# ScalarE copies the last unit's transposed probabilities before, not after, the exponentials of the third slot of a pair

## The chip, the cores and the metric

The kernel runs on one core of one Trainium2 chip. The metric is the device time of one execution, in microseconds (us); lower is better. Three runs of the kernel before took 1274.99, 1270.4 and 1275.39 us, so the median is 1274.99 us.

## The reference, cut to what matters

The input holds 4 sequences of 512 rows with 512 columns. Each goes through a half-weighted feed-forward step, an attention step, and the same feed-forward step again:

```python
x = x + 0.5 * ffn(layernorm(x))     # W_base, plus low-rank experts weighted by a softmax
x = x + attention(layernorm(x))
x = x + 0.5 * ffn(layernorm(x))

# attention, 32 heads, causal, latent width 64
scores = (q_lat @ c_kv.T + q_rope @ k_rope.T) / sqrt(192)    # lower triangle only
probs = softmax(scores)
out = (probs @ c_kv) @ w_uv[h]      # per head, then concatenated
return out @ w_out
```

Nearly all of the time is in the attention step. All of it is float32 in and out; the kernel computes most products from a high and a low part of each operand.

## The kernel before, in words

For each of the four sequences (the loop variable `b`; the first three run in a hardware loop, the fourth is written out after it), `attend` works through 16 pairs of heads, then `last_outputs` and `steps` do the rest. The scores of one pair of heads make five **units** (`MEMBERS`), each of at most 512 columns of one PSUM bank: unit 0 and unit 1 are the last 128 rows of head 0 and head 1 (512 columns each), units 2 and 3 are 384 + 128 columns of one head each, and unit 4 is 256 + 256 columns, one of each head. So a sequence has 80 **slots** `u`, five to a pair, with `k = u % 5`. I call the slot with k = 2 the third slot, and the one with k = 3 the fourth.

What one unit goes through: TensorE computes its scores (`scores`, L849 to L851); VectorE adds the mask and takes the negated maximum (L1490); ScalarE takes the exponentials and their sum (L1120); VectorE inverts the sum (`inverse_sums`, L1445); GpSimd multiplies the unit's probabilities by it (L576); three slots later (`T_LAG = 3`) TensorE transposes the unit into a PSUM bank (`transpose_probs`, L870); and ScalarE or VectorE copies that bank to `probT` in SBUF (`copy_probT`: L367 on ScalarE for units 0, 2 and 4, L369 on VectorE for units 1 and 3). Because of the lag of three slots, unit 4 of a pair is transposed and copied in the third slot of the next pair, beside that pair's unit 2. In the fourth slot TensorE multiplies all of the pair's `probT` by `ckv` (`pv`, L885, 20 matmuls).

All engines run their instructions in the order written, and wait on semaphores. In the third slot the orders are:

- TensorE: scores of unit 2; the query products of head 1 of the next pair (`q_products`, L834); the transposes of the old unit 4. In the fourth slot: scores of unit 3; `pv`; the transposes of unit 0. In the fifth: scores of unit 4, transposes of unit 1, and six matmuls of the output projection (`output`, L911).
- ScalarE: `qT_high` (L1091, the high part of the next queries of head 0); the exponentials of unit 2; the copy of the old unit 4. In the fourth slot: exponentials of unit 3, copy of unit 0.
- VectorE: mask and maximum of unit 2, `inverse_sums` of unit 1, three products for the rotary embedding of the queries (L1436 to L1438). In the fourth slot: mask of unit 3, then `inverse_sums` of unit 2.
- GpSimd: `q_sum` (L496), scaling of unit 2 (L576); in the fourth slot `qT_low` (L501) and the scaling of unit 3.

The waits that matter here. `pv` waits for all five copies of its pair (`probT_by_act`, `probT_by_dve`) and for `oT_hi_set` and `oT_lo_set` of the pair before. The copy waits for `probT_done`, which the last transpose of the unit sets, and for `pv_done` of the pair before. The exponentials of unit `u` wait for `neg_max_set` (VectorE) and for the transposes of unit `u - 4`, whose buffer they overwrite. The scores of unit `u + 2` wait for the exponentials of unit `u` (`prob_set`), whose PSUM bank they overwrite. The exponentials' instructions are one ACTIVATE and one ACTIVATION_READ_ACCUMULATOR per member of the unit.

Of the kernel before, what the change touches and what calls it, by code (L numbers as in the profile page):

```python
# [58 lines left out]
UNITS = 5  # L59
# [13 lines left out]
T_LAG = 3  # L73
# [6 lines left out]
ACT_BANKS = (0, 2, 4)  # L80
# [27 lines left out]
def build(nc, hidden, w_q_down, w_q_up_nope, w_q_up_rope, w_kv_down, w_k_rope, w_uk, w_uv, w_out,  # L108
          W_base, b_base, lora_A, lora_B, router_W, router_b, domain_prior, active,
          rope_cos, rope_sin, rope_cosT, rope_sinT, out):  # L110
    with ExitStack() as ctx:
# [206 lines left out]
        def attention(slot_work, tail):  # L318

            for g in range(BODIES):  # L320
                for u in range(BODY + (tail if g == BODIES - 1 else 0)):
                    slot_work(g, u)

        def known(g, u, least):

            return not isinstance(g, int) or BODY * g + u >= least

        def within(g, u, most):

            return not isinstance(g, int) or BODY * g + u <= most  # L330
# [15 lines left out]
        def probT_unit(v):  # L346

            k = v % UNITS
            if k == UNITS - 1:
                return probT[:].rearrange("p (h s) q -> p h s q", h=2)[:, :, 2:6:3, :]  # L350
            at = HEAD_BLOCKS * (k % 2) + k // 2
            return probT[:, at:at + 10:3, :]

        def bank_unit(v):

            if v % UNITS == UNITS - 1:
                return probT_ps[v % 2].rearrange("p (h s q) -> p h s q", h=2, s=2)
            return probT_ps[v % 2].rearrange("p (s q) -> p s q", s=4)

        def copy_probT(eng, do, b, g, v):  # L360

            pair = 16 * b + BODY_PAIRS * g + v // UNITS
            eng.wait_ge(probT_done, 80 * b + BODY * g + v + 1)
            if known(g, v, UNITS):
                eng.wait_ge(pv_done, pair)
            if eng.engine == nc.scalar.engine:
                do.activation(probT_unit(v), bank_unit(v), ACT.Copy).then_inc(probT_by_act, 1)  # L367
            else:
                do.tensor_copy(probT_unit(v), bank_unit(v)).then_inc(probT_by_dve, 1)  # L369
# [4 lines left out]
        def q_index(b, n, head):  # L374

            return 34 * b + 2 + 2 * n + head

        SLOTS = UNITS * PAIRS
        LAST_PAIR = PAIRS - 1

        with nc.Block() as block:
# [574 lines left out]
            def _(act):  # L956
# [132 lines left out]
                def qT_high(m, head, par, cols=slice(0, S)):  # L1089
                    act.wait_ge(q_sum_set, m + 1)  # L1090
                    nc.scalar.activation(qT_hi[par][:, head, cols], q_sums[par][:, head, cols],  # L1091
                                         ACT.Copy).then_inc(qT_hi_set, 1)

                def oT_high(b, g, p):

                    q = p - 2
                    act.wait_ge(pv_done, 16 * b + BODY_PAIRS * g + q + 1)
                    if q % 2 == 0 and known(g, UNITS * q, 4 * UNITS):
                        act.wait_ge(y_ps, 32 * b + ST * ((BODY_PAIRS // 2) * g + q // 2 - 1))
                    elif q % 2 == 1 and known(g, UNITS * q, 3 * UNITS):  # L1100
                        act.wait_ge(y_ps, 32 * b + ST * ((BODY_PAIRS // 2) * g + q // 2))
                    nc.scalar.activation(oT_hi[oT_buffer(q)][:], o_ps, ACT.Copy).then_inc(oT_hi_set, 1)

                def attend(b):
                    def work(g, u):
                        k, p = u % UNITS, u // UNITS
                        n1 = BODY_PAIRS * g + p + 1
                        queries = within(g, u, UNITS * LAST_PAIR - 1)
                        if k == 0 and known(g, u, 2 * UNITS):
                            oT_high(b, g, p)  # L1110
                        if k in (2, 4) and queries:
                            qT_high(q_index(b, n1, k // 2 - 1), k // 2 - 1, (p + 1) % 2)
                        if within(g, u, SLOTS - 1):
                            n = 80 * b + BODY * g + u
                            act.wait_ge(neg_max_set, n + 1)
                            if known(g, u, RING):
                                act.wait_ge(probT_done, n - RING + 1)
                            for m, (_, i, c) in enumerate(MEMBERS[k]):
                                w = (i + 1) * P
                                last = nc.scalar.activation(prob[u % RING][:, c:c + w], score_ps[u % 2][:, c:c + w],  # L1120
                                                            ACT.Exp, bias=neg_max[:, u % RING, m:m + 1], scale=-1.0,
                                                            accum_out=row_sum[:, u % RING, m:m + 1])
                            last.then_inc(prob_set, 1)
                        v = u - T_LAG
                        if known(g, u, T_LAG) and within(g, u, SLOTS - 1 + T_LAG) and v % UNITS in ACT_BANKS:
                            copy_probT(act, nc.scalar, b, g, v)
                    attention(work, TAIL)

# [410 lines left out]
```

## Time and profile before

| What | Value |
|---|---|
| Median of the three runs | 1274.99 us |
| The profiled execution's own time | 1273.67 us |
| Its span, first to last instruction | 1271.8 us |
| Mean granted TensorE clock | 0.969 of full speed |
| TensorE matmul (PE) busy | 1132.7 us (89%) |
| VectorE (DVE) busy | 935.7 us (74%) |
| ScalarE (ACT) busy | 597.7 us (47%) |
| GpSimd (POOL) busy | 740.3 us (58%) |

The page calls TensorE's matmuls PE, its weight loads PEld, VectorE DVE, ScalarE ACT and GpSimd POOL; L885 is line 885 of the kernel. The attention steps of the four sequences take roughly 400 to 620 us, and so on: one such step is about 210 us long, and its 16 `pv` are 14 us apart for most of it. A busy share says little by itself: the matmuls' ends are modelled, and a matmul overlaps the next by about 0.16 us, so that two matmuls with nothing between them stand in the trace with a slightly negative gap. The idle time before an instruction is given in square brackets, with who ended it.

### The profile page before, as it was taken

The numbers are of one execution on the slowest core, as the hardware profiler recorded it, in microseconds if no ns is written. First come the engines' busy times: TensorE is split into PE (matmuls) and PEld (weight loads), VectorE is DVE, ScalarE is ACT, GpSimd is POOL, SyncE is SP. The second block draws the span as 40 slices with busy tenths as digits, with TensorE's granted clock in tenths as the row PEclk, the third lists the DMA queues.
The fourth block names the chain that finished last, engine by engine and source line by source line (L and its number), as shares of the span: only waits on it lengthen the run. The fifth ranks groups of instructions, "written<-read, shape, count | busy, mean of one in ns | idle before, by whom it ended". The sixth has DMA issues, their size and how long they took to land.

```text
span 1271.8 us, 24129 instructions
## 1 busy us (share of the span) xinstructions
PE 1132.7 (89%) x7312; PEld 935.6 (74%) x7312; DVE 935.7 (74%) x3049; ACT 597.7 (47%) x1698; POOL 740.3 (58%) x943
## 2 busy tenths in 40 slices
PE   5978899999897899999887889999989689999996
PEld 4646777777695777777686677777769567777776
DVE  4767778886676877887667777788667668878855
ACT  3645555555133555555323455555512355555541
POOL 1417877776214877777303777777721387777741
PEclk9999999999898999999989999999989899999998
DMA  9740000000100000000100000000000000000000
GB/s 264 204 137 1 2 1 1 2 1 2 33 34 2 2 1 1 2 1 1 35 34 2 1 2 1 1 1 1 1 34 34 2 1 1 2 1 1 1 1 34
DMA packets 21674, 28.00 MB, mean 22 GB/s; under 512 B 10247, under 2 KB 12039, under 8 KB 20907
## 3 DMA queue, kind: packets, MB, share of 16 engines
q1 hardware_dynamic: 19178, 21.71, 5.5%
q10 hardware_dynamic: 2368, 4.72, 1.2%
q8 instruction: 65, 1.06, 0.4%
q14 instruction: 63, 0.51, 0.1%
HBM read 22.23 MB, written 4.19 MB: 21 GB/s over the span
## 4 chain that ended last, share of the span: by engine, by line
PE 50%; DVE 20%; issue 16%; ACT 6%; POOL 5%; SPq 1%; DMA 1%; DVEq 0%; ACTq 0%; POOLq 0%
PE Y L885 10%; PE Y L911 9%; PE XZ L870 6%; PE Y L616 5%; PE XZ L616 4%; PE Y L834 3%; DVE XZ L1490 3%; DVE q_turned L1437 3%; ACT prob L1120 3%; DVE q_sums L1436 3%; DVE probT L369 2%; PE XZ L849 2%; ACT probT L367 2%; PE XZ L851 2%; PE XZ L850 2%
## 5 line engine op out<-in xcount | busy, mean ns | idle before, releaser
L1120 ACT ACTIVATE prob<-XZ,small 128x512 f32<-128x512 f32 (+3 forms) x512 | 266.5, 525 | 344.3 <-DVE small L1490 343.9
L576 POOL TENSOR_TENSOR prob<-prob,small 128x512 f32<-128x512 f32 (+3 forms) x512 | 360.3, 721 | 63.6 <-DVE small L1445 47.1
L1490 DVE CUSTOM_DVE_ANT_0 XZ<-XZ,mask 128x512 f32<-128x512 f32 (+3 forms) x512 | 245.1, 510 | 162.3 <-issue 160.0
L496 POOL TENSOR_TENSOR q_sums<-q_sums,q_turned 64x512 f32<-64x512 f32 (+2 forms) x136 | 165.2, 1215 | 163.4 <-DVE q_turned L1438 159.6
L501 POOL TENSOR_TENSOR qT_lo<-q_sums,qT_hi 128x512 fp32r<-128x512 f32 (+2 forms) x136 | 166.0, 1221 | 79.6 <-ACT qT_hi L1091 79.6
L870 PE MATMUL XZ<-ident,prob 128*128 128x128 f32 x1280 | 196.0, 276 | 5.1 <-POOL prob L576 4.8
L885 PE MATMUL Y<-probT,ckv 128*64 128x384 f32 (+2 forms) x1280 | 155.6, 390 | 48.0 <-ACT probT L367 48.0
L849 PE MATMUL XZ<-kT_hi,qT_hi 128*128 128x512 f32 (+3 forms) x512 | 178.5, 349 | 17.3 <-POOL qT_lo L501 11.2
L870 PEld LDWEIGHTS XZ<-ident,prob 128*128 128x128 f32 x1280 | 150.2, 140 | 44.1 <-issue 14.4
L885 PEld LDWEIGHTS Y<-probT,ckv 128*64 128x64 f32 x1280 | 92.1, 139 | 105.6 <-issue 62.9
L850 PE MATMUL XZ<-kT_lo,qT_hi 128*128 128x512 f32 (+3 forms) x512 | 166.9, 326 | 0.0
L851 PE MATMUL XZ<-kT_hi,qT_lo 128*128 128x512 f32 (+3 forms) x512 | 166.7, 326 | 0.0
L367 ACT ACTIVATE probT<-XZ 128x512 f32<-128x512 f32 x192 | 114.6, 597 | 63.2 <-PE XZ L870 62.3
L849 PEld LDWEIGHTS XZ<-kT_hi,qT_hi 128*128 128x128 f32 x512 | 98.1, 192 | 27.6 <-ACT prob L1120 11.3
L1449 DVE TENSOR_TENSOR x_sb<-Y,x_sb 128x512 f32<-128x512 f32 x128 | 88.0, 687 | 35.1 <-PE Y L911 34.3
L911 PE MATMUL Y<-wo_hi,oT_hi 128*128 128x512 f32 x256 | 110.9, 433 | 1.6 <-DVE x_sb L1449 1.4
L470 POOL TENSOR_TENSOR var_eps<-moments,small 128x1 f32<-128x1 f32 (+3 forms) x26 | 5.2, 201 | 176.7 <-DVE moments L1152 176.7
L850 PEld LDWEIGHTS XZ<-kT_lo,qT_hi 128*128 128x128 f32 x512 | 98.7, 193 | 5.0
L851 PEld LDWEIGHTS XZ<-kT_hi,qT_lo 128*128 128x128 f32 x512 | 98.1, 192 | 5.7
L1120 ACT ACTIVATION_READ_ACCUMULATOR prob<-XZ,small 128x1 f32 x512 | 100.8, 197 | 1.0 <-issue 1.0
L911 PE MATMUL Y<-wo_hi,oT_lo 128*128 128x512 f32 x256 | 101.0, 395 | 0.0
L911 PE MATMUL Y<-wo_lo,oT_hi 128*128 128x512 f32 x256 | 100.3, 392 | 0.0
(199 smaller groups left out, 2300.2 us busy)
## 6 DMA issues: line engine op xcount, KB each, us to landing
wout_nat<-in_L_attn_w_out_dram SPq DMA_DIRECT2D x16, 512.0 KB, 4.3
out_dram<-x_sb SPq DMA_DIRECT2D x16, 256.0 KB, 2.0
x_next<-_attn_hidden_states_dram SPq DMA_DIRECT2D x12, 256.0 KB, 3.6
wbase_nat<-in_L_ffn_W_base_dram ACTq DMA_DIRECT2D x1, 1024.0 KB, 5.4
x_sb<-_attn_hidden_states_dram ACTq DMA_DIRECT2D x4, 256.0 KB, 6.8
nope_a<-_L_attn_w_q_up_nope_dram ACTq DMA_DIRECT2D x1, 1024.0 KB, 7.0
rope_a<-_L_attn_w_q_up_rope_dram SPq DMA_DIRECT2D x1, 1024.0 KB, 8.8
rope_bb<-_L_attn_w_q_up_rope_dram SPq DMA_DIRECT2D x2, 512.0 KB, 11.4
```

Of the source, the lines that this page charges most:

```text
L367: do.activation(probT_unit(v), bank_unit(v), ACT.Copy).then_inc(probT_by_act, 1)
L496: nc.gpsimd.tensor_tensor(q, q, turned, ALU.add).then_inc(q_sum_set, 1)
L501: nc.gpsimd.tensor_tensor(qT_lo[par][:, head, cols], q_sums[par][:, head, cols], f32(qT_hi[par][:, head, cols]), ALU.subtract).then_inc(qT ...
L576: last = nc.gpsimd.tensor_tensor(prob[u % RING][:, c:c + w], prob[u % RING][:, c:c + w], inv_sum[:, u % RING, m:m + 1].broadcast_to([P, w] ...
L849: nc.tensor.matmul(bank[:, c:c + w], high, kT_hi[:, 0:w], start=True, stop=False)
L850: nc.tensor.matmul(bank[:, c:c + w], high, kT_lo[:, 0:w], start=False, stop=False)
L851: last = nc.tensor.matmul(bank[:, c:c + w], low, kT_hi[:, 0:w], start=False, stop=True)
L870: last = nc.tensor.transpose(probT_ps[v % 2][:, at], prob[v % RING][:, at], ident[:])
L885: last = nc.tensor.matmul(o_ps[64 * h:64 * h + 64, column * P:(column + n) * P], ckv[:, j, :], probT[:, HEAD_BLOCKS * h + at:HEAD_BLOCKS * ...
L911: last = nc.tensor.matmul(bank, o[buffer][:, rows], w, start=(k == 0 and j == 0), stop=(k == 1 and j == 2))
L1120: last = nc.scalar.activation(prob[u % RING][:, c:c + w], score_ps[u % 2][:, c:c + w], ACT.Exp, bias=neg_max[:, u % RING, m:m + 1], scale= ...
L1490: last = nc.vector.tensor_tensor_reduce(bank, bank, mask[:, S - w:S], -1.0, HIGHEST, ALU.add, ALU.min, neg_max[:, u % RING, m:m + 1])
```

## The change

In `attend` of ScalarE the condition for the copy is computed before the exponentials. If the slot is a third slot (k = 2), the copy is issued there, before the exponentials of unit 2; in the other slots that have one (k = 0 and k = 3) it stays behind the exponentials. Nothing else is changed: the same instructions with the same waits are issued, and only ScalarE's order of two of them in 15 of the 16 third slots of each sequence differs (the first third slot has no copy; the one after the last pair has no exponentials).

```diff
                         if k in (2, 4) and queries:
                             qT_high(q_index(b, n1, k // 2 - 1), k // 2 - 1, (p + 1) % 2)
+                        v = u - T_LAG
+                        copies = known(g, u, T_LAG) and within(g, u, SLOTS - 1 + T_LAG) and v % UNITS in ACT_BANKS
+                        if copies and k == 2:
+                            copy_probT(act, nc.scalar, b, g, v)
                         if within(g, u, SLOTS - 1):
                             n = 80 * b + BODY * g + u
                             act.wait_ge(neg_max_set, n + 1)
...
                             last.then_inc(prob_set, 1)
-                        v = u - T_LAG
-                        if known(g, u, T_LAG) and within(g, u, SLOTS - 1 + T_LAG) and v % UNITS in ACT_BANKS:
+                        if copies and k != 2:
                             copy_probT(act, nc.scalar, b, g, v)
```

## Rows read from the trace of the kernel before

**Rows 1.** Chain of waits, 445 to 475 us: start us, us, what it was.

```profile
458.99 0.49 ACT probT L367
459.49 0.23 issue
459.71 2.38 PE Y L885 x20
...
463.83 1.41 PE Y L911 x6
465.26 0.05 DVE x_sb L1449
...
471.95 0.19 DVE XZ L1490
...
473.98 1.05 PE Y L885 x7
```

**Rows 2.** Who waited for whom, whole span: us in total, times, longest.

```profile
PE Y L885 <- ACT probT L367: 48.0, 60, 1.8
```

**Rows 3.** The same view, 418 to 626 us (second sequence).

```profile
PE Y L885 <- ACT probT L367: 12.4, 15, 1.4
```

**Rows 4.** The same view, 1028 to 1234 us (fourth sequence).

```profile
PE Y L885 <- ACT probT L367: 10.8, 15, 1.8
```

**Rows 5.** Timeline of PE, 457.5 to 463: start us, us, instruction, [idle before <-releaser].

```profile
457.61 0.60 PE L870 MATMUL XZ<-ident,prob 128*128 128x128 f32 x4
...
458.74 0.27 PE L851 MATMUL XZ<-kT_hi,qT_lo 128*128 128x128 f32 x1
459.71 2.38 PE L885 MATMUL Y<-probT,ckv 128*64 128x384 f32 x20 [0.70 <-ACT probT L367]
462.02 0.66 PE L870 MATMUL XZ<-ident,prob 128*128 128x128 f32 x4
```

**Rows 6.** Timeline of ACT, 457 to 463.

```profile
456.65 0.62 ACT L1091 ACTIVATE qT_hi<-q_sums 128x512 fp32r<-128x512 f32 x1
457.97 0.58 ACT L1120 ACTIVATE prob<-XZ,small 128x384 f32<-128x384 f32 x1 [0.70 <-DVE small L1490]
...
458.88 0.59 ACT L367 ACTIVATE probT<-XZ 128x512 f32<-128x512 f32 x1
...
461.81 0.20 ACT L1120 ACTIVATION_READ_ACCUMULATOR prob<-XZ,small 128x1 f32 x1
462.80 0.60 ACT L367 ACTIVATE probT<-XZ 128x512 f32<-128x512 f32 x1 [0.79 <-PE XZ L870]
```

**Rows 7.** Timeline of DVE, 450 to 464.3.

```profile
452.38 0.67 DVE L1497 TENSOR_TENSOR oT_lo<-Y,oT_hi 128x512 fp32r<-128x512 f32 x1
...
455.87 0.67 DVE L369 COPY probT<-XZ 128x512 f32<-128x512 f32 x1
...
460.81 0.16 DVE L1445 RECIPROCAL small<-small 128x2 f32<-128x2 f32 x1
463.44 0.43 DVE L1490 CUSTOM_DVE_ANT_0 XZ<-XZ,mask 128x256 f32<-128x256 f32 x1 [2.47 <-issue]
```

**Rows 8.** Timeline of POOL, 450 to 472.

```profile
461.46 1.18 POOL L576 TENSOR_TENSOR prob<-prob,small 128x384 f32<-128x384 f32 x2 [0.16 <-POOL q_sums L496]
```

**Rows 9.** Timelines of ACT, then PE, 428 to 433 (second pair of a sequence).

```profile
429.45 0.62 ACT L1091 ACTIVATE qT_hi<-q_sums 128x512 fp32r<-128x512 f32 x1
...
431.08 0.59 ACT L367 ACTIVATE probT<-XZ 128x512 f32<-128x512 f32 x1
...
431.92 0.87 PE L885 MATMUL Y<-probT,ckv 128*64 128x384 f32 x4 [1.24 <-ACT probT L367]
```

**Rows 10.** Timelines of PE, then ACT, 1068.1 to 1070.5 (fourth sequence).

```profile
1068.18 0.60 PE L870 MATMUL XZ<-ident,prob 128*128 128x128 f32 x4
...
1070.11 0.87 PE L885 MATMUL Y<-probT,ckv 128*64 128x384 f32 x4 [0.51 <-ACT probT L367]
...
1069.46 0.59 ACT L367 ACTIVATE probT<-XZ 128x512 f32<-128x512 f32 x1
```

## The prediction

> **What bounds the kernel now.** I read the page first: TensorE is busy 89% of the span and no other engine over 74%, so the question is what TensorE's idle time waits for. The view of who waited for whom answers it for the edited place: the largest wait of a matmul on another engine is that of `pv` (L885) on ScalarE's copy (L367), 48.0 us in 60 waits [rows 2]. Sixty is four sequences times fifteen, just the third slots in which a copy and exponentials both stand. The chain of waits, read next, shows that this wait is on the path: in every 14.27 us (from `pv` at 459.71 to the next at 473.98) it runs copy, 0.23 us of issue, `pv`, TensorE up to the output matmuls, then VectorE from the output's addition (465.26) to the mask of unit 2 (471.95), the exponentials of unit 2, and the copy again [rows 1]. So the old period of a pair is a loop through VectorE, and what ties VectorE into it is only that the exponentials of unit 2, which need VectorE's mask, stand ahead of the copy on ScalarE. The copy itself doesn't need them.
>
> The timelines give the place in one steady pair. The transposes of the old unit 4 end at 457.61 + 0.60 = 458.21; the fourth slot's last score matmul ends at 458.74 + 0.27 = 459.01; `pv` starts at 459.71 with 0.70 us of idle time before it [rows 5]. ScalarE is free from 456.65 + 0.62 = 457.27, starts the exponentials at 457.97, when VectorE's maximum is there, and the copy only at 458.88; it ends at 459.47, and `pv` follows 0.24 us later [rows 6]. I take 44 of the 60 pairs as like this one, eleven a sequence; the other four waits of each sequence are longer, as the sum of 12.4 us for fifteen says: 12.4 - 11 x 0.70 = 4.7 us, 1.2 each [rows 3].
>
> **The change, part by part.** Nothing is added or removed; the same instructions with the same waits are issued, and no DMA and no queue is passed. Two things move.
>
> *The copy comes earlier.* It now waits for the transposes (458.21) and for `pv_done`, long set. What ScalarE needs after a transpose the other copy of the pair shows, that of unit 0, which already waits for TensorE: transposes end at 462.02 + 0.66 = 462.68, copy starts at 462.80, so 0.12 us [rows 5, 6]. Start 458.33, end 0.59 later at 458.92, `pv` 0.24 later at 459.16. The other conditions of `pv` are there: VectorE's copy of unit 3 ended at 456.54, the low half of the previous output at 453.05 [rows 7]. TensorE is ready too: 459.16 is 0.15 us after the modelled end of the last score matmul, where 0.70 stood. Gain 0.55 us a steady pair. This 0.12 us is the one cost that the trace shows only elsewhere; its bounds are nothing below and, above, the 0.24 us that `pv` takes after a copy; so 0.43 to 0.67 a pair. I keep 0.12, since the row is of the same instruction with the same two waits.
>
> *The exponentials of unit 2 come later.* ScalarE's instructions overlap by about 0.1 us when back to back, which is also why 458.88 follows 457.97 by only 0.91; so they start at about 458.82 and not at 457.97, 0.85 later, and end at about 459.84. Who waits for them: VectorE's `inverse_sums` of unit 2 runs at 460.81, behind the rotary products and the mask of unit 3 which don't need them [rows 7], so 0.97 us of cover; GpSimd's scaling at 461.46 follows that [rows 8]; TensorE's scores of unit 4 come behind `pv` and the transposes, after 462.02 + 0.66 - 0.55 = 462.13 [rows 5]; ScalarE's own exponentials of unit 3 wait for VectorE's mask, whose last reading precedes 460.81. Cost nothing. If the cover were gone, each 0.1 us over it would be 0.1 us a pair.
>
> *What is late next.* Relative to the start of `pv`, everything TensorE issues afterwards moves with it, and with that VectorE's next mask and addition. What does not move is VectorE's and ScalarE's work for the fourth slot. So I ask for each how short a period P it allows. The copy's own loop: 14.27 - 0.55 = 13.72. TensorE with no wait: idle 0.70 plus the overlap of two matmuls, about 0.16, taken out, 13.41. The exponentials of unit 3 end at 461.81 + 0.20 = 462.01, the copy of unit 0 starts at 462.80 [rows 6]: 0.79 of cover, 13.48. VectorE: it is done with the fourth slot at 460.97 and starts the fifth's mask at 463.44, 2.47 us idle [rows 7], so 11.8. GpSimd's scaling of unit 2 ends at 462.64 [rows 8] and TensorE transposes it over four us later, in the pair's successor. None of them reaches 13.72, so the whole 0.55 stays.
>
> *The other pairs.* In the second pair of a sequence ScalarE is held by VectorE and GpSimd before the third slot's exponentials: `qT_high` ends at 430.07, the copy started at 431.08 and `pv` at 431.92 with 1.24 us idle [rows 9]. The copy would start some 0.1 before 430.07, at 429.97, end at 430.56, and `pv` come at 430.80; the idle time becomes 0.12. So 0.15 us of idle time is left there as well, and I count all fifteen waits of a looped sequence alike: 12.4 - 15 x 0.15 = 10.15 us [rows 3]; three sequences give 30.4.
>
> *The fourth sequence* is written out, and `pv` follows the copy after 1070.11 - (1069.46 + 0.59) = 0.06 us [rows 10]. Transposes end at 1068.78; copy to 1069.4 or 1069.5, `pv` at 1069.5 or 1069.55, which is what TensorE could do at the earliest: the whole idle time of 0.51 goes and some of the overlap comes back. That is 10.8 us [rows 4] and up to 15 x 0.07 more; its longest wait, 1.8 us, stands out from the others and may have a cause that a reorder does not remove, so I take 11.1.
>
> **Sum.** 30.4 + 11.1 = 41.5 us. The profiled execution took 1273.67 us, its span 1271.8; 1273.67 - 41.5 = 1232.2. It lies 1.3 us below the median of the runs, which is within their spread; I predict 1232.
>
> **A rule that speaks against it.** The timeline shows that ScalarE does not pass a waiting instruction: the copy of unit 0 waits 0.79 us for its transposes, and nothing of the next slot is run meanwhile [rows 6]. The Trainium skill, "TensorE: Matmul & The Clock Gate", section "Architectural detail: the array is 16× 32×32, not 1× 128×128", says that of ScalarE and VectorE: their queues are strictly first in, first out, and only TensorE may pull weight loads ahead. By that rule the exponentials now wait behind a copy that waits for TensorE, wherever TensorE is late; the third rival below prices it.
>
> **The rivals.**
>
> *Forecast, 0.80:* `pv` starts about 0.55 us earlier in steady pairs, over a microsecond earlier in the pairs at both ends; 1228 to 1239 us.
>
> *Part of it, 0.13:* the gain of the steady pairs is there, but the longer waits of the other sixteen pairs turn into waits elsewhere, since there VectorE and GpSimd, and not TensorE, set the pace before the third slot. For it: ScalarE's `qT_high` ends a microsecond after the transposes in the second pair [rows 9], a sign that TensorE isn't the late one there. Against: after `pv` those engines are fed by TensorE again. Then 44 x 0.56 = 25 us: 1249.
>
> *Nothing, 0.04:* another condition of `pv` is late by as much, and the wait only changes its name. Against it are the two ends of rows 7, 2.6 us and more ahead. 1273.
>
> *Slower, 0.03:* the exponentials of unit 2 become the path. The place is VectorE's `inverse_sums` of unit 2 in the fourth slot, then GpSimd's scaling, then TensorE's transposes of unit 2. It decides from the point at which the copy ends more than 0.97 us later than I have it, that is after 459.9. A copy held that long gives `pv` no gain, and the exponentials' own move of 0.85 would stand in the loop: if 0.4 us of it a pair came through after what `pv` gains, 60 x 0.4 = 24 us, 1298. Against: the transposes end 0.24 us after the exponentials' old start, and four us lie between GpSimd's scaling and its reader.
>
> **How the numbers follow.** The forecast's own spread is 0.43 to 0.67 a pair and what the ends of the sequences give: 1228 to 1239. The range goes on toward the partial case, up to 1246, and to 1227 below, where ScalarE follows TensorE at once; outside is most of the partial case and the two small ones, under 2 in 10. No change here can be told from one of under 0.5%, 6.4 us. Faster by more than that: 0.80 + 0.13 = 0.93. Same: 0.04. Slower: 0.03.
>
> **What the changed profile would show.** In a steady pair the copy stands ahead of the exponentials of unit 2, starts 0.1 us after the fourth transpose and has an idle time put down to PE L870; `pv` waits 0.15 us or less, too short to be listed much, so that the 48.0 us of `pv` on the copy fall below 10; `pv` of two neighbouring pairs lie 13.7 us apart (13.5 in the fourth sequence). The chain of waits leaves VectorE and stays on TensorE, with the transposes and the copy in it. VectorE's idle time before L1490 in the fifth slot shrinks from 2.47 to about 1.9. The exponentials of unit 2 end near 459.84 on the old time scale, and `inverse_sums` behind them doesn't wait. It would be wrong if `pv` had a new wait of over 0.3 us, if the period stayed above 14, or if `inverse_sums` waited for ScalarE in steady pairs.

## The result, and the profile after

The changed kernel takes 1224.98 us (median of four runs, 1224.57 to 1225.95). The kernel before, run beside it, takes 1274.08 us (1270.4 to 1275.39). The ratio is 0.962, with a 95% interval of 0.9598 to 0.9642: about 49 us faster. I had forecast 1232 and a range of 1227 to 1246, so the direction was right and the time lies 2 us below the lower end. The profiled execution took 1225.95 us with a span of 1224.1; its counterpart of before had 1273.67 and 1271.8. So the two traces differ by 47.7 us, and that is what has to be explained against my sum of 41.5.

The page of the kernel after: the busy lines of its first part, the shares of the chain that ended last, and the group of `pv`.

```profile
PE 1129.4 (92%) x7312; PEld 933.0 (76%) x7312; DVE 936.0 (76%) x3049; ACT 597.5 (49%) x1698; POOL 741.1 (61%) x943
...
PE 78%; DVE 7%; POOL 6%; issue 5%; ACT 2%; DMA 1%; SPq 1%; POOLq 0%; DVEq 0%; ACTq 0%
...
L885 PE MATMUL Y<-probT,ckv 128*64 128x384 f32 (+2 forms) x1280 | 152.3, 383 | 3.2 <-issue 0.9
```

TensorE's share of the chain rose from 50% to 78%, VectorE's fell from 20% to 7%. The 48.0 us that `pv` waited for ScalarE's copy [rows 2] are gone from the view of who waited for whom. What stands there now is the copy waiting for TensorE, its own reason for coming late. (This view put 62.3 us in 64 waits of the copy down to TensorE before already, nearly all of them for unit 0's; in the steady pairs of the loop unit 0's wait has shrunk from 0.79 to 0.15 us, and unit 4's has come in, 0.97 us each.)

```profile
ACT probT L367 <- PE XZ L870: 67.1, 80, 1.9
```

In the new file the lines below 1115 are moved by three or four: the exponentials are L1124, VectorE's mask is L1493, `inverse_sums` L1448. The timeline of PE at the pair that answers to [rows 5]:

```profile
458.04 0.60 PE L870 MATMUL XZ<-ident,prob 128*128 128x128 f32 x4
...
459.17 0.27 PE L851 MATMUL XZ<-kT_hi,qT_lo 128*128 128x128 f32 x1
459.50 2.38 PE L885 MATMUL Y<-probT,ckv 128*64 128x384 f32 x20
461.81 0.66 PE L870 MATMUL XZ<-ident,prob 128*128 128x128 f32 x4
```

The same pair in the timeline of ACT, which answers to [rows 6]:

```profile
457.08 0.62 ACT L1091 ACTIVATE qT_hi<-q_sums 128x512 fp32r<-128x512 f32 x1
458.67 0.60 ACT L367 ACTIVATE probT<-XZ 128x512 f32<-128x512 f32 x1 [0.97 <-PE XZ L870]
459.17 0.58 ACT L1124 ACTIVATE prob<-XZ,small 128x384 f32<-128x384 f32 x1
...
459.97 0.21 ACT L1124 ACTIVATION_READ_ACCUMULATOR prob<-XZ,small 128x1 f32 x1
461.41 0.58 ACT L1124 ACTIVATE prob<-XZ,small 128x384 f32<-128x384 f32 x1 [1.23 <-DVE small L1493]
...
462.58 0.60 ACT L367 ACTIVATE probT<-XZ 128x512 f32<-128x512 f32 x1 [0.15 <-PE XZ L870]
```

The transposes end at 458.04 + 0.60 = 458.64 and the copy starts at 458.67, 0.03 us later (0.04 in most pairs). `pv` comes 0.24 us after the copy's end, as before, and 0.06 us after the last score matmul's end (459.44) instead of 0.70. The exponentials of unit 2 end at 459.97 + 0.21 = 460.18. The timeline of DVE, answering to [rows 7], shows that nobody waits for them:

```profile
461.24 0.16 DVE L1448 RECIPROCAL small<-small 128x2 f32<-128x2 f32 x1
463.23 0.43 DVE L1493 CUSTOM_DVE_ANT_0 XZ<-XZ,mask 128x256 f32<-128x256 f32 x1 [1.83 <-issue]
```

`inverse_sums` starts 1.06 us after the last reading and has no idle time before it. VectorE's idle time ahead of the fifth slot's mask went from 2.47 to 1.83 us, which is the 0.64 that the pair got shorter. The chain of waits, 445 to 475 us, which answers to [rows 1]:

```profile
445.88 2.38 PE Y L885 x20
...
458.20 0.44 PE XZ L870 x4
...
459.50 2.38 PE Y L885 x20
...
463.62 1.39 PE Y L911 x6
```

From `pv` to `pv` it is 459.50 - 445.88 = 13.62 us, where 14.27 stood, and every piece between is TensorE's; no row of VectorE or ScalarE is left in it. Over 14 us of this stretch (columns: length, then busy time and count of PE, PEld, DVE, ACT, POOL, granted clock, DMA share, GB/s) TensorE is busy for 13.94:

```profile
459.00:473.00 14.00, 13.94 (x90) 11.56 (x89) 11.64 (x38) 8.22 (x24) 11.03 (x14) 1.00 0.01 2
```

Taken from the end of the first pair's transposes to the start of the last `pv`, the four attention steps became shorter like this (us):

| Sequence | before | after | gain | less 1.53 or 1.48 of low clock (below) | my sum |
|---|---|---|---|---|---|
| 1 | 208.32 | 197.38 | 10.94 | 10.94 | 10.15 |
| 2 | 208.35 | 197.21 | 11.14 | 11.14 | 10.15 |
| 3 | 210.00 | 197.03 | 12.97 | 11.44 | 10.15 |
| 4 | 208.15 | 194.88 | 13.27 | 11.79 | 11.1 |

That is 48.3 us; 0.6 went the other way outside these stretches, 0.47 of it ahead of the first attention step, where nothing was changed. The 6.2 us above my sum are thus 3.8 in the pairs themselves, 3.0 of low clock, and -0.6.

**The low clock.** In the trace of before TensorE's granted clock falls to 0.50 (1.2 instead of 2.4 GHz) twice within an attention step, each time just behind a long wait of `pv`. The windows of the kernel before over both places:

```profile
735.40:738.70 3.30, 3.30 (x18) 1.94 (x14) 0.67 (x5) 1.02 (x4) 2.59 (x4) 0.50 0.00 0
1028.90:1032.30 3.40, 3.40 (x19) 1.70 (x15) 0.00 (x0) 0.58 (x4) 2.05 (x3) 0.50 0.02 5
```

And its timeline of PE at the first of them:

```profile
734.82 4.06 PE L885 MATMUL Y<-probT,ckv 128*64 128x384 f32 x20 [1.23 <-ACT probT L367]
```

The same 20 matmuls take 4.06 us instead of 2.38. From the first to the last of them it is 3.64 us there and 3.59 at 1028.3, where every other `pv` has 2.11: 1.53 + 1.48 = 3.0 us. That is a lower bound, since the work behind `pv` is slowed too: the period behind the first of them is 15.20 us, where the other two looped sequences have 13.53, so 1.7 us; for the second there is no undisturbed neighbour to compare.

From a sequence's first `pv` to its last, the trace of after has no such stretch. Ahead of the fourth sequence's first `pv`, while TensorE computes that sequence's first scores, it has one. TensorE had waited there for ScalarE and for GpSimd, and not in a `pv`:

```profile
978.83 0.44 PE L849 MATMUL XZ<-kT_hi,qT_hi 128*128 128x384 f32 x1 [1.20 <-ACT prob L1124]
...
980.82 0.78 PE L870 MATMUL XZ<-ident,prob 128*128 128x128 f32 x4 [0.92 <-POOL prob L576]
```

```profile
981.30:984.60 3.30, 3.13 (x14) 2.74 (x13) 1.97 (x12) 1.73 (x6) 3.14 (x4) 0.50 0.00 0
```

The trace of before has none at that place, but a longer one (10.2 us instead of 6.8) just ahead of it. So the low clock isn't bound to waits of `pv`. Where I count low stretches below, I mean those that begin at a sequence's first `pv` or later, since these are the ones that the change can have removed.

### The profile page after: what moved, and what is told of

It is laid out like the page before. It is cut to its first block, busy times and chain, and to the rows that moved or that the text cites. A ratio compares the mean times of both kernels' runs of the same rounds, so it can differ in the third digit from the quotient of the medians.

```text
span 1224.1 us, 24129 instructions
## 1 busy us (share of the span) xinstructions
PE 1129.4 (92%) x7312; PEld 933.0 (76%) x7312; DVE 936.0 (76%) x3049; ACT 597.5 (49%) x1698; POOL 741.1 (61%) x943
## 3 DMA queue, kind: packets, MB, share of 16 engines
q8 instruction: 65, 1.06, 0.4%
## 4 chain that ended last, share of the span: by engine, by line
PE 78%; DVE 7%; POOL 6%; issue 5%; ACT 2%; DMA 1%; SPq 1%; POOLq 0%; DVEq 0%; ACTq 0%
PE Y L911 14%; PE Y L885 11%; PE XZ L870 11%; PE Y L834 11%; PE XZ L851 6%; PE XZ L850 6%; PE XZ L849 5%; PE Y L616 5%; PE XZ L616 4%; POOL prob L576 2%; POOL q_sums L496 2%; PE XZ L595 2%; POOL qT_lo L501 2%; DVE q_turned L1440 1%; DVE stats L1151 1%
## 5 line engine op out<-in xcount | busy, mean ns | idle before, releaser
L1124 ACT ACTIVATE prob<-XZ,small 128x512 f32<-128x512 f32 (+3 forms) x512 | 266.6, 526 | 290.6 <-DVE small L1493 289.2
L1493 DVE CUSTOM_DVE_ANT_0 XZ<-XZ,mask 128x512 f32<-128x512 f32 (+3 forms) x512 | 245.0, 510 | 114.5 <-issue 112.2
L885 PE MATMUL Y<-probT,ckv 128*64 128x384 f32 (+2 forms) x1280 | 152.3, 383 | 3.2 <-issue 0.9
L1124 ACT ACTIVATION_READ_ACCUMULATOR prob<-XZ,small 128x1 f32 x512 | 101.7, 199 | 0.0
```

The source lines that it names most:

```text
L885: last = nc.tensor.matmul(o_ps[64 * h:64 * h + 64, column * P:(column + n) * P], ckv[:, j, :], probT[:, HEAD_BLOCKS * h + at:HEAD_BLOCKS * ...
L1493: last = nc.vector.tensor_tensor_reduce(bank, bank, mask[:, S - w:S], -1.0, HIGHEST, ALU.add, ALU.min, neg_max[:, u % RING, m:m + 1])
```

## The experiments

My theory after the result: only the order on ScalarE matters; each of the sixty waits of `pv` gives what stood in it; and the excess is (a) ScalarE following a transpose at once, (b) the low clock behind the long waits, now gone. Rivals: that the longer waits at the ends of a sequence give all of the excess, that the order of the exponentials matters as well, or that the gain is one of TensorE's order. The short diffs are against the kernel after, unless said otherwise. Each run is compared with the kernel before on the same chip.

### Only the steady pairs, and only the others

```diff
-                        if copies and k == 2:
+                        early = k == 2 and 4 <= BODY_PAIRS * g + p <= 14
+                        if copies and early:
...
-                        if copies and k != 2:
+                        if copies and not early:
```

> The copy stands ahead of the exponentials only in the third slots of pairs 4 to 14 (eleven waits of pv a sequence), and behind them in pairs 1, 2, 3 and 15. Theory: the gain is made pair by pair where the copy follows the transposes at once, 0.62 to 0.64 us a pair in the three looped sequences and 0.57 in the fourth, so 33 x 0.63 + 11 x 0.57 = 27 us, 1247; the low-clock stretches of TensorE that begin at 735 and 1029 us of the kernel before, each right behind a long wait of pv, can still occur. Rival (all of the excess over the 41.5 us of the prediction comes from the steady pairs): 33 us or more, 1241 or less.

```diff
-                        if copies and k == 2:
+                        early = k == 2 and not 4 <= BODY_PAIRS * g + p <= 14
+                        if copies and early:
...
-                        if copies and k != 2:
+                        if copies and not early:
```

> The complement: early copy only in pairs 1, 2, 3 and 15 of each sequence. Theory: 49.1 - 27 = 22 us, 1252, of which 0.8 + 1.1 + 1.0 + 1.35 = 4.2 us a sequence (17 us in all) are waits of pv and the other 5 are the two low-clock stretches and one stall of ScalarE at 1027 us, which need a long wait of pv before them and are gone. Rival (part of the ends' gain is given back elsewhere): 17 us or less, 1257 or more.

The first took 1248.78 us (1246.76 to 1250.13), ratio 0.979 (0.9765 to 0.9814), -27.2 us; the second 1253.13 us (1252.58 to 1254.99), ratio 0.9829 (0.9806 to 0.9853), -22.8 us. Together that is 50.0, and the whole change brought 49.1: the parts add up, neither needs the other. So the partial rival falls: the longer waits of the other sixteen pairs gave more a pair than the steady ones (22.8 / 16 = 1.4, the low clock included, against 27.2 / 44 = 0.62), and nothing of them turned into a wait elsewhere.

The low clock goes with the long waits. The kernel with only the steady pairs changed keeps those at the beginning of a sequence, and keeps two low stretches in its fourth sequence; its windows there, and the `pv` ahead of the first in its timeline of PE:

```profile
1009.40:1012.80 3.40, 3.40 (x19) 1.93 (x16) 0.00 (x0) 0.00 (x0) 1.37 (x3) 0.50 0.00 0
1023.10:1026.40 3.30, 3.30 (x18) 1.69 (x16) 1.01 (x7) 1.02 (x4) 2.97 (x4) 0.50 0.00 0
```

```profile
1008.37 1.66 PE L885 MATMUL Y<-probT,ckv 128*64 128x384 f32 x10 [2.04 <-ACT probT L367]
```

The complement, which keeps the forty-four waits of 0.5 to 0.7 us and no long one, has none. (Both kernels have one ahead of the fourth sequence's first `pv`, as the kernel after has.)

### The kernel before, profiled once more

> The kernel before once more, for its profile alone. Theory: the steady pairs repeat to 0.05 us (period 14.27 and 14.08, 0.70 and 0.51 us of idle time before pv), while low-clock stretches of TensorE behind a long wait of pv (1.2 us or more, pairs 1, 2, 3 and 15 of a sequence) come at other places or in another number, none to four of them, each 1.5 us. Rival (they belong to fixed places of the program): again at pair 1 of the third and the first pv of the fourth sequence.

It took 1275.13 us (one run). Its steady pairs repeat to the hundredth: 14.27 us, and 14.08 in the fourth sequence. The low stretches don't. There are three, and of the two of the first profile one recurs:

```profile
432.00:435.40 3.40, 3.33 (x14) 1.81 (x16) 1.26 (x7) 1.02 (x4) 3.08 (x4) 0.51 0.00 0
1029.30:1032.70 3.40, 3.40 (x20) 1.89 (x16) 0.00 (x0) 0.00 (x0) 1.44 (x3) 0.50 0.02 5
1042.90:1046.30 3.40, 3.40 (x16) 1.61 (x18) 1.28 (x7) 1.02 (x4) 3.24 (x4) 0.51 0.00 0
```

Its span is 1273.3 against 1271.8 us, 1.5 more, about the price of the one stretch more, though other pieces differ as well (the fourth sequence's first wait is 2.11 us here and was 1.77). In the three profiles that show such stretches (the kernel before twice, and the one with only the steady pairs changed) thirteen waits of `pv` are over a microsecond. The longest, that of the fourth sequence's first pair (1.8 to 2.1 us), has a low stretch behind it in all three; of the other thirty-six (1.0 to 1.5 us) four do, and not the same ones each time. The kernel before varies by 5 us between its runs and the kernel after by 1.4; stretches that come and go would do that, but of the kernel before only two runs were profiled. Not every such difference is explained by them: one unprofiled run of the kernel of the next section took 5.2 us more than its three others.

### The late wait last

`pv` waits for four semaphores, and between the copy's end and `pv` lie 0.24 us. In the order of the changed kernel's instructions the wait that ends last, that for ScalarE's copy, doesn't stand at the matmul but on a register instruction ahead of it, which computes the next threshold:

```
L877 REGISTER_ALU
L878 REGISTER_ALU [waits probT_by_act]
L881 EVENT_SEMAPHORE [waits oT_lo_set,oT_hi_set]
L885 MATMUL [waits probT_by_dve]
```

The trace shows the chain in full: the copy ends at 459.27, the register instruction (L878) starts at 459.31, the one that only waits (L881) at 459.40, the first weight load at 459.47, the matmul at 459.50. I moved the waits so that the late one comes last:

```diff
-                    pe.wait_ge(probT_by_act, by_act)
-                    pe.wait_ge(probT_by_dve, by_dve)
                     if known(g, UNITS * p, UNITS):
                         pe.wait_ge(oT_hi_set, pair)
                         pe.wait_ge(oT_lo_set, pair)
+                    pe.wait_ge(probT_by_dve, by_dve)
+                    pe.wait_ge(probT_by_act, by_act)
```

> The changed kernel, with the four waits of pv in another order: the one for ScalarE's copies stands last and not first. Theory: in the loop pv follows the copy 0.24 us later because three more waits against register values are looked at behind the one that is late (0.13 us in the first pair of a sequence, which has one more only; 0.05 where the values are constants). With the late one last pv follows within 0.13 us, 0.1 us or a little more a looped pair is gained until TensorE runs back to back: 45 x 0.12 = 5 us, 1220. Rival (the 0.24 us is the semaphore's own travel): no change, 1225.

It took 1220.44 us (1220.39 to 1225.65), ratio 0.9583 (0.9553 to 0.9613). That is the fastest median of all kernels here, 4.5 us below the changed one. The intervals of the two against before overlap, so the step over the changed kernel rests on the traces: spans of 1218.6 and 1224.1, and this timeline of PE.

```profile
443.02 0.27 PE L851 MATMUL XZ<-kT_hi,qT_lo 128*128 128x128 f32 x1
443.23 0.97 PE L885 MATMUL Y<-probT,ckv 128*64 128x384 f32 x6
```

`pv` starts 0.06 us before the modelled end of the last score matmul, back to back, and the looped pairs take 13.49 us, just what the fourth sequence, where thresholds are constants, had at once after the change. `pv` follows the copy there after 0.11 us, with TensorE busy until then, and after 0.06 in each looped sequence's second pair.

The fourth sequence itself lost by it. The same order in the source puts the late wait elsewhere there:

```
L881 EVENT_SEMAPHORE [waits probT_by_act,oT_lo_set]
L885 MATMUL [waits oT_hi_set]
```

```profile
1023.48 0.27 PE L851 MATMUL XZ<-kT_hi,qT_lo 128*128 128x128 f32 x1
1023.73 0.98 PE L885 MATMUL Y<-probT,ckv 128*64 128x384 f32 x6
```

The copy ends at 1023.59 and `pv` follows after 0.14 us. The steady period of this sequence is 13.53 us, where the changed kernel, with the late wait on the matmul, has 13.49. So a wait that is written last doesn't always stand on the work. One of the four runs took 1225.65 us, the other three 1220.39 to 1220.45; it was not profiled, and I can't say why.

### TensorE's order in place of ScalarE's

From the kernel before, with ScalarE as it was: the transposes of unit 0 ahead of `pv`, so that TensorE works while it would wait.

```diff
-                        if k == PV_SLOT and known(g, u, UNITS):
-                            pv(b, g, p - 1)
...
+                        if k == PV_SLOT and known(g, u, UNITS):
+                            pv(b, g, p - 1)
```

> The kernel before, with TensorE's transposes of unit 0 ahead of pv in the fourth slot and not behind it; ScalarE's order is the old one. Theory (the old period is a loop copy, pv, TensorE, VectorE's mask, exponentials of unit 2, copy): 0.35 us of TensorE's work moves out of that loop into its wait, the period falls from 14.27 to 13.92, and the kernel by 44 x 0.35 and as much in the other pairs, 15 to 21 us: 1253 to 1259. Rival (TensorE's idle time before pv is cover for something else that is late): no change, 1274.

It took 1239.68 us (1238.98 to 1240.31), ratio 0.9722 (0.97 to 0.9744), -36.3 us: a miss, as I had expected 1253 to 1259. So there is a second way to most of this gain, from TensorE's side. Its timelines of PE and of ACT say why it gave more than I had:

```profile
448.71 0.62 PE L870 MATMUL XZ<-ident,prob 128*128 128x128 f32 x4
449.39 0.54 PE L885 MATMUL Y<-probT,ckv 128*64 128x384 f32 x2
```

```profile
448.74 0.59 ACT L367 ACTIVATE probT<-XZ 128x512 f32<-128x512 f32 x1
```

The transposes fill 0.39 us of the wait, where I had 0.35. But `pv` also follows the copy (449.33) after 0.06 us and not 0.24. In this order the late wait, that for ScalarE's copy, sits on the matmul itself; the other three end on instructions ahead of it. The period is 14.27 - 0.39 - 0.19 = 13.69 us, as measured. That holds for the three looped sequences: 42 x 0.19, and 0.08 in the first pair of each, are 8.2 us. In the fourth `pv` followed the copy after 0.05 us before already, and there the period fell by the 0.39 alone. This trace also lacks the two low stretches of before, 3.0 us or a little more. With 60 x 0.39 = 23.4 that makes 34.6 us, and the two traces differ by 34.7. My expectation had only the first of the three terms, at 0.35 and less. The sum takes all pairs alike, so that it comes out this near is in part luck.

### How much cover the exponentials have

The change delays the exponentials of unit 2. To see what that may cost, they are computed again, once or three times more, each time with a wait for the repetition before; the result stays the same.

```diff
+                            extra = 1 if copies and k == 2 else 0    # 3 in the second kernel
+                            for again in range(extra + 1):
...
+                                if again < extra:
+                                    last.then_inc(exps_repeated, 1)
+                                    act.wait_ge(exps_repeated, extra * (15 * b + BODY_PAIRS * g + p - 1) + again + 1)
```

> The changed kernel, with the exponentials of unit 2 computed twice in every third slot that has a copy, the second time with the same result and behind a wait for the first; so prob_set for unit 2 comes one set of exponentials, 1.0 to 1.2 us, later. Theory (in a steady pair their reader, VectorE's inverse_sums, comes 1.06 us after them): at most 0.15 us a pair on VectorE, which has 1.8 us of idle time behind it, and nothing on the path: 1225, within 3. Rival (a late exponential of unit 2 is on the path at once): 60 x 1.0 = 60 us, 1285.

> The same with the exponentials of unit 2 computed four times: prob_set 3.0 to 3.6 us later, at about 463.2 to 463.8 on the scale where the scores of unit 4 start at 462.23. Theory: the scores of unit 4 wait for them, 1.0 to 1.6 us a pair, and ScalarE's exponentials of unit 3 and its copy of unit 0 are late behind them; 60 x 1.0 to 2.0 = 60 to 120 us, 1285 to 1345. Rival (ScalarE has time enough, being busy 49%): 1225.

Once more: 1225.01 us (1224.7 to 1225.41), ratio 0.9601 (0.9585 to 0.9618), no difference from the kernel after. Its timelines of ACT and DVE (its lines are moved by three to six):

```profile
460.25 0.20 ACT L1127 ACTIVATION_READ_ACCUMULATOR prob<-XZ,small 128x1 f32 x1
...
460.48 0.17 DVE L1454 RECIPROCAL small<-small 128x2 f32<-128x2 f32 x1
```

The cover of 1.06 us is just used up: the last reading ends at 460.45 and `inverse_sums` starts at 460.48. Three times more: 1298.48 us (1298.2 to 1298.77), ratio 1.0177 (1.0159 to 1.0195), 73.5 us over the kernel after. Its waits, and its timeline of PE:

```profile
DVE small L1454 <- ACT prob L1127: 122.0, 63, 3.0
```

```profile
470.70 0.39 PE L850 MATMUL XZ<-kT_hi,qT_hi 128*128 128x256 f32 x1 [0.93 <-ACT prob L1127]
```

So the slower rival's mechanism is real. Past the cover `inverse_sums` is late, and TensorE's scores of unit 4 wait for the PSUM bank of unit 2; the period is 14.83 us. It needs more than one microsecond of delay beyond what the change brings.

### The fourth slot's copy ahead too

```diff
-                        if copies and k == 2:
+                        if copies and k in (2, 3):
...
-                        if copies and k != 2:
+                        if copies and k not in (2, 3):
```

> The changed kernel, with the copy of unit 0 also ahead of the exponentials of unit 3 in the fourth slot. There the copy waits for transposes that stand behind pv, so that the exponentials of unit 3 start 1.6 us later, at about 463.08 for 461.41. Theory: VectorE's inverse_sums of unit 3 and the copy of unit 0 as before, then qT_high 1.0 us later, and with it GpSimd's qT_low and scaling of unit 3, whose cover before the transposes is 1.6 us: 1225 to 1235, not faster. Rival (the earlier a copy the better): 1215 to 1222.

It took 1230.76 us (1229.93 to 1230.78), ratio 0.9646 (0.9629 to 0.9663), so it gains nothing over the kernel after and seems to lose some 5 us. Its waits, the timeline of ACT, and that of PE:

```profile
ACT probT L367 <- PE XZ L870: 203.7, 120, 2.7
```

```profile
423.84 0.60 ACT L367 ACTIVATE probT<-XZ 128x512 f32<-128x512 f32 x1 [2.41 <-PE XZ L870]
```

```profile
425.40 0.50 PE L849 MATMUL XZ<-kT_hi,qT_hi 128*128 128x512 f32 x1 [0.53 <-ACT prob L1124]
```

Here the copy stands in the queue for 2.41 us before its transposes are done, and the exponentials of unit 3, which were ready, stand behind it. Where the pairs have little slack, at the beginning of a sequence, TensorE's next scores then wait for them. The first two periods of the second sequence are 12.19 and 13.10 us instead of 11.81 and 12.51, and its last two 11.95 and 10.60 instead of 11.62 and 10.43; the steady ones stay at 13.63. This is the rule that I had cited from the Trainium skill, "TensorE: Matmul & The Clock Gate", section "Architectural detail: the array is 16× 32×32, not 1× 128×128": ScalarE and VectorE work their queues strictly in order. The trace agrees. It costs something in this kernel and nothing in the changed one, whose copy waits 0.97 us in a steady pair with nothing ready behind it for which anyone is waiting.

## Why the prediction was right, and where its size was wrong

The mechanism came as forecast, and the time did not: 1224.98 us lies below the range. Two terms of the sum were at fault. One is the 0.12 us that a copy needs after its transposes, which measured 0.04 here, so that a steady pair gained 0.64 us and not 0.55. The other is TensorE's clock, about 3 us, which the sum left out.

**The bound, and what to move: right.** `pv` waited for a copy that stood behind exponentials it didn't need; the wait went in all sixty pairs, and the chain left VectorE, as forecast. The two halves of the change add up to the whole.

**"What ScalarE needs after a transpose the other copy of the pair shows": the step that failed.** I took 0.12 us from the copy of unit 0, and kept it "since the row is of the same instruction with the same two waits". The waits are the same two, but they don't sit in the same place. ScalarE's instructions at the two copies, which are so in the kernel before already:

```
unit 0:  L365 REGISTER_ALU [waits probT_done]
         L367 ACTIVATE probT<-XZ [waits pv_done]
unit 4:  L365 EVENT_SEMAPHORE [waits pv_done]
         L367 ACTIVATE probT<-XZ [waits probT_done]
```

For unit 0 the late wait, that for the transposes, ends on a register instruction, which computes the threshold of the other wait, and only then comes the copy. In the trace of before they start at 462.72 and 462.80, 0.08 us apart. Unit 4's copy carries the late wait itself. In one pair of the kernel after both can be read: transposes end at 458.64 and 462.47, copies start at 458.67 and 462.58, 0.03 and 0.11. That it is the place of the wait and not the unit, the fourth sequence shows. There the thresholds are constants, and unit 0's copy carries the wait for its transposes itself. It starts 0.04 us after them in the steady pairs, in the kernel before too, and the lines could have been read ahead of the change. Its timelines of PE and ACT:

```profile
1072.41 0.66 PE L870 MATMUL XZ<-ident,prob 128*128 128x128 f32 x4
...
1073.11 0.60 ACT L367 ACTIVATE probT<-XZ 128x512 f32<-128x512 f32 x1 [0.52 <-PE XZ L870]
```

So a steady pair gained 0.64 and not 0.55, 7.0 us a sequence and not 6.05. My lower bound of "nothing" held this case, and I took the other row as the nearer one. TensorE's side gave the same answer: 0.24 between copy and `pv` became 0.06 to 0.11 where the late wait came to stand on the matmul.

**"So 0.15 us of idle time is left there as well": close.** In the second pair 0.11 was left in two of the looped sequences and 0.15 in the first. Three more pairs of the first and two of the second show 0.1 us more than their neighbours; I have no cause for these. The first pair kept nothing (`pv` 0.05 before the modelled end). The pairs outside the steady eleven gave 4.4 us in the third sequence where my sum has 4.1.

**The sum has no term for TensorE's clock: missing.** I read [rows 5] at full clock and forgot what a wait of 1.2 us does to the work behind it. The two stretches are worth at least 3.0 of the 6.2 us. The trace of before showed both, in its granted clock and in a `pv` of 4.06 us. That they stood behind the very waits the change removes was to be seen; that they would go with them is likely from the runs, but not shown (see the last section).

**The fourth sequence, "I take 11.1": too cautious.** Its longest wait, 1.8 us, "may have a cause that a reorder does not remove". The cause is a pause of ScalarE amid its exponentials, before, in its timeline of ACT:

```profile
1027.57 0.20 ACT L1120 ACTIVATION_READ_ACCUMULATOR prob<-XZ,small 128x1 f32 x1 [1.01 <-issue]
1027.68 0.58 ACT L367 ACTIVATE probT<-XZ 128x512 f32<-128x512 f32 x1
```

After, in the same slot:

```profile
991.20 0.60 ACT L367 ACTIVATE probT<-XZ 128x512 f32<-128x512 f32 x1
...
993.63 0.37 ACT L1124 ACTIVATE prob<-XZ,small 128x128 f32<-128x128 f32 x1 [1.27 <-issue]
```

The pause is still there and even longer, but the copy is now ahead of it, and it costs nothing. With the low clock left out, this sequence gave 11.79: all of the 10.8 of its waits, and 15 overlaps of some 0.07. What the pause is, I have not tested; it stands in the first written-out pair after the loop.

**What is late next: right.** The copy's loop sets the period, 13.63 where my 0.12 gave 13.72, and with the late wait last TensorE's own work sets it, 13.49 where I had 13.41. The exponentials' cover is 1.06 us where I had 0.97, and the experiments bound it from both sides. GpSimd and VectorE had the room I gave them.

**The range.** Its lower end of 1227 was to take in ScalarE following TensorE at once, but left no room for the clock beside it. Either excess alone would have left the time inside: 1224.98 + 3.0 is 1228.0, and 1224.98 + 3.8 is 1228.8.

## What to carry to other kernels

When an in-order engine has one item that the critical engine waits for and one that it doesn't, put first the one that is waited for, then check that nothing is ready behind it for longer than the other's cover; here the cover was 1.06 us and the gain 0.64 a pair. When a latency after a wait is taken from another row of the same instruction, look at the instructions between wait and work as well. Put the wait that ends last where it stands on the work itself, and look in the instructions whether it does: last in the source did it in the loop and undid it in the written-out sequence. When a change removes waits of TensorE of over a microsecond, look up the granted clock behind them and price the slower work too.

## What the runs showed of the hardware

- **Instructions behind a wait.** A register instruction between the late wait and the work costs about 0.08 us. With it ScalarE's copy follows its transposes after 0.11 to 0.12, without it after 0.03 to 0.04. TensorE's `pv` follows the copy after 0.24 us where the late wait is on a register instruction and one that only waits stands between, after 0.13 to 0.14 where it is on one instruction ahead of the matmul, and after 0.05 to 0.06 where it is on the matmul (0.11 where TensorE was itself busy until then).
- **The clock behind a wait.** The granted clock went to 0.50 for 3.4 us beginning within about 1 us of the end of single waits of `pv` of 1.0 to 2.1 us, where TensorE was busy before and after. By the periods, with an undisturbed one beside them, four of the seven cost 1.6 to 1.7 us each. None of the waits of 0.5 to 0.8 us did it, 47 in each profile of before. Of the long ones few did: seven of thirty-nine in three profiles, and one of 1.60 us in the kernel with TensorE's order changed left the clock at 1.00. The Trainium skill, "TensorE: Matmul & The Clock Gate", section "HAM oscillation — how this bites in real kernels", describes idle time between groups of matmuls that makes the next group start at half clock. The trace agrees that it happens, though behind few of these waits.
- **What speaks against the wait as the whole cause.** That the waits cause it is an association over ten profiles: the seven without long waits of `pv`, or with that single one, show no low stretch behind a sequence's first `pv`. But in one of the seven, that with the exponentials computed three times more, TensorE's scores wait over a microsecond for ScalarE in eighteen pairs (1.04 to 1.10 us, fifteen of them in the fourth sequence), and the clock stays at 1.00 behind all of them. And seven of the ten profiles have a low stretch of 3.4 us amid the fourth sequence's first scores, where no `pv` waits. No run changed a wait's length alone, so how long a wait must be, and what else it takes, stays open. The first of the fifteen, in its timeline of PE:

```profile
1048.91 0.38 PE L850 MATMUL XZ<-kT_hi,qT_hi 128*128 128x256 f32 x1 [1.06 <-ACT prob L1127]
```
